# A two-batch model of six sublayers on one core: gate product of the feed-forward that runs beside the recurrence, moved from GpSimd to VectorE

## The reference

```python
x = x + 0.5 * ffn(layernorm(x))      # FFN0
x = x + mamba(layernorm(x))          # d_inner 512, d_state 16
x = x + 0.5 * ffn(layernorm(x))      # FFN1
x = x + 0.5 * moe(layernorm(x)); x = x + attention(layernorm(x)); x = x + 0.5 * moe(layernorm(x))

def ffn(x):                          # W1, W3: 1024 x 256, W2: 256 x 1024
    hidden = silu(x @ W1.T) * (x @ W3.T)
    return fwht(hidden) @ W2.T       # the transform is folded into W2 by the kernel
```

## Time and profile before

| | |
|---|---|
| runs | 899.51, 901.68, 901.64 us, median 901.64 |
| the profiled execution | 899.96 us, its span 897.9 us |
| TensorE busy | 761.5 us (85%) |
| VectorE busy | 570.1 us (63%) |
| ScalarE busy | 411.5 us (46%) |
| GpSimd busy | 270.1 us (30%) |
| mean granted clock of TensorE | 0.953 |

### The profile page before, as it was taken

The page is one execution under the profiler, slowest core; times in us unless marked ns, Lnnn a source line. Parts: engine busy times, 40 slices in busy tenths (PEclk is TensorE's granted clock), DMA queues, the critical chain, the costliest instruction groups (busy, mean ns, idle before and its releaser), DMA issues.

```text
span 897.9 us, 11226 instructions
## 1 busy us (share of the span) xinstructions
PE 761.5 (85%) x4027; PEld 531.3 (59%) x4027; DVE 570.1 (63%) x973; ACT 411.5 (46%) x606; POOL 270.1 (30%) x200
## 2 busy tenths in 40 slices
PE   3998868885793788898999999997789998685997
PEld 2688544552461355557787777774457785344776
DVE  4654698998959989984556556358524546713543
ACT  3455687664238466643332333440475431263221
POOL 0002069986503878980797000001000010000000
PEclk9999989998996989999999999999999999897999
DMA  9200011221101122215101000043000241000000
GB/s 297 76 1 1 2 58 59 82 71 59 47 1 49 58 59 75 79 59 155 63 2 20 1 1 1 13 108 93 4 1 1 66 115 32 28 1 0 1 1 24
DMA packets 30669, 41.88 MB, mean 47 GB/s; under 512 B 3817, under 2 KB 20019, under 8 KB 30579
## 3 DMA queue, kind: packets, MB, share of 16 engines
q1 hardware_dynamic: 29222, 40.41, 15.1%
q10 hardware_dynamic: 1396, 0.79, 0.4%
HBM read 36.83 MB, written 4.36 MB: 46 GB/s over the span
## 4 chain that ended last, share of the span: by engine, by line
PE 51%; DVE 16%; issue 14%; ACT 8%; DMA 5%; POOL 3%; SPq 2%; DVEq 0%; ACTq 0%; POOLq 0%
PE PS L462 34%; DVE PS L1706 3%; PE PS L776 2%; DVE shared L1714 2%; PE PS L912 2%; POOL shared L2014 2%; ACT shared L1332 2%; DMA route<-scratch_c 2%; PE PS L727 2%; PE PS L810 2%; DMA scratch_k<-shared 2%; ACT shared L1281 1%; DVE route L1765 1%; SPq L1953 1%; PE PS L655 1%
## 5 line engine op out<-in xcount | busy, mean ns | idle before, releaser
L2014 POOL TENSOR_TENSOR shared<-shared,route 128x1024 f32<-128x1024 f32 x64 | 151.8, 2376 | 105.0 <-DVE shared L1714 102.7
L462 PE MATMUL PS<-xnT,weights_r 128*128 128x256 f32 (+1 forms) x744 | 162.2, 365 | 11.3 <-ACT shared L1036 7.4
L462 PE MATMUL PS<-xnT,work_r 128*128 128x512 f32 (+1 forms) x624 | 159.1, 406 | 0.0
L462 PE MATMUL PS<-weights_r,work_r 128*128 128x256 f32 (+1 forms) x1008 | 147.3, 295 | 5.5 <-POOL work_r L1980 3.7
L1714 DVE TENSOR_TENSOR_SCAN shared<-shared,PS 128x512 f32<-128x512 f32 x128 | 148.8, 1203 | 4.0 <-POOL shared L2014 3.8
L462 PEld LDWEIGHTS PS<-xnT,weights_r 128*128 128x128 f32 x744 | 120.1, 194 | 46.1 <-issue 28.6
L462 PEld LDWEIGHTS PS<-weights_r,work_r 128*128 128x128 f32 (+1 forms) x1008 | 128.1, 191 | 24.5 <-issue 15.7
L1481 DVE TENSOR_TENSOR gated<-gated,PS 128x512 f32<-128x512 f32 (+1 forms) x68 | 46.6, 686 | 136.8 <-ACT gated L1016 136.8
L462 PEld LDWEIGHTS PS<-xnT,work_r 128*128 128x128 f32 (+1 forms) x624 | 115.8, 191 | 29.2 <-issue 1.1
L776 PE MATMUL PS<-shared,cf 128*128 128x512 f32 x256 | 128.0, 625 | 1.7 <-POOL shared L2014 1.7
L1016 ACT ACTIVATE gated<-PS 128x512 f32<-128x512 f32 (+1 forms) x68 | 40.6, 597 | 177.6 <-PE PS L462 170.7
(11 more groups left out here) (188 smaller groups left out, 949.9 us busy)
## 6 DMA issues: line engine op xcount, KB each, us to landing
route<-scratch_c SPq DMA_DIRECT2D x64, 256.0 KB, 3.1
shared<-in_L_ffn_W_dram SPq DMA_DIRECT2D x3, 1024.0 KB, 13.1
scratch_k<-shared SPq DMA_DIRECT2D x12, 128.0 KB
scratch_q<-shared SPq DMA_DIRECT2D x12, 128.0 KB
shared<-scratch_k SPq DMA_DIRECT2D x8, 192.0 KB
shared<-scratch_q SPq DMA_DIRECT2D x8, 192.0 KB
mamba_w<-in_L_ffn_w_dram SPq DMA_DIRECT2D x2, 704.0 KB, 5.2
beside<-in_L_ffn_w_dram SPq DMA_DIRECT2D x2, 704.0 KB, 7.9
```

The source lines that it names most:

```text
L462: last = nc.tensor.matmul(o, lhs[l], rhs[r], start=(start and i == 0), stop=(stop and i == 2))
L2014: nc.gpsimd.tensor_tensor(hc[:, u * 2 * T:(u + 1) * 2 * T].rearrange("p (c t) -> p c t", c=2), hst[:, (t % 2) * 2 * T:(t % 2 + 1) * 2 * T] ...
```

## The change

The gate product of all 16 units is done by VectorE, with the linear part read straight from bank 1. ScalarE's copy into `side_lin` and the tensor itself are gone. The SiLU counts a new semaphore `silu`, for which VectorE's product waits; TensorE's next unit waits for the product (`prod`) where it waited for the copy. The wait for the down product of unit i-2 moves from the copy to the rounding. VectorE's product stands at step u+2, ahead of that step's products and scans; for units 0 and 1 of the first phase it stands in front of and behind `norm_low`, and for the last two units where VectorE already had it. GpSimd keeps the remainders.

```diff
@@ TensorProgram.side_up
                 if r == 0:
                     pe.wait_ge(xnT_ev, 2 * it + 2)
-                    pe.wait_ge(f["lin"], b * UNITS + i)
+                    pe.wait_ge(f["prod"], b * UNITS + i)
@@ ScalarProgram
                 if i >= 2:
                     act.wait_ge(*side_done(b, i - 2, "hid"))
-                nc.scalar.activation(gated[:, (i % 2) * T:(i % 2 + 1) * T], bank(SIDE_GATE), ACT.Silu)
+                nc.scalar.activation(gated[:, (i % 2) * T:(i % 2 + 1) * T], bank(SIDE_GATE), ACT.Silu)\
+                    .then_inc(f["silu"], 1)
+
+            def side_high(self, b, i):
+
+                act, f = self.act, F
+                act.wait_ge(f["prod"], b * UNITS + i + 1)
                 if i >= 2:
                     act.wait_ge(*side_used(b, i - 2))
-                nc.scalar.activation(side_lin[i % RING], bank(SIDE_LIN), ACT.Copy).then_inc(f["lin"], 1)
-
-            def side_high(self, b, i):
-
-                act, f = self.act, F
-                act.wait_ge(*side_done(b, i, "prod"))
@@ VectorProgram.side_prod
-                self.dve.wait_ge(F["lin"], b * UNITS + i + 1)
-                nc.vector.tensor_tensor(g, g, side_lin[i % RING], ALU.mult).then_inc(F["prod_late"], 1)
+                self.dve.wait_ge(F["silu"], b * UNITS + i + 1)
+                nc.vector.tensor_tensor(g, g, bank(SIDE_LIN), ALU.mult).then_inc(F["prod"], 1)
@@ VectorProgram.mamba
                     self.norm(0, it + 1)
+                    self.side_prod(0, 0)
                     self.norm_low(it + 1, 0, banks=(2, 3))
+                    self.side_prod(0, 1)
                     self.taps(0, range(EC))
...
                 for t in range(STEPS):
+                    for i in range(2 * (1 - b), UNITS):
+                        if step_of(b, up_end(i)) + 2 == t:
+                            self.side_prod(b, i)
...
+                for i in range(ON_VECTOR):
+                    if step_of(b, up_end(i)) + 2 >= STEPS:
+                        self.side_prod(b, i)
@@ GpSimd, mamba
                     for i in range(2):
-                        side_prod(0, i)
                         side_low(0, i)
...
                         if step_of(b, up_end(i)) + 3 == t:
                             side_low(b, i)
-                        if step_of(b, up_end(i)) + 1 == t:
-                            side_prod(b, i)
```

More of the change, by code:

```diff
@@ L218, in build @@
         WoT, a = cut(shared, a, DC * D)
-        side_lin = [shared[:, RING_AT + i * 2 * T + T:RING_AT + (i + 1) * 2 * T] for i in range(RING)]
         ring = [halves(RING_AT + i * 2 * T, T)[0] for i in range(RING)]
@@ L330, in build @@
                                       "dA", "mul", "scan", "hc", "ys", "yr", "yf0", "yf"))
-        F = {n: sem(f"side_{n}") for n in ("up", "lin", "prod", "high", "hid", "used", "down", "res", "prod_late", "hid_late")}
+        F = {n: sem(f"side_{n}") for n in ("up", "silu", "prod", "high", "hid", "used", "down", "res", "hid_late")}
         SIDE_STAGE, SIDE_BATCH = (FFN0, FFN1), (1, 0)
@@ L1981, in side_low @@
                     .then_inc(f["hid"], 1)
-            def side_prod(b, i):
-                g = gated[:, (i % 2) * T:(i % 2 + 1) * T]
-                pool.wait_ge(F["lin"], b * UNITS + i + 1)
-                nc.gpsimd.tensor_tensor(g, g, side_lin[i % RING], ALU.mult).then_inc(F["prod"], 1)
             def mamba(b):
@@ L2034, in mamba @@
                     for i in range(ON_VECTOR):
-                        if step_of(b, up_end(i)) + 1 >= STEPS:
-                            side_prod(b, i)
                         if step_of(b, up_end(i)) + 3 >= STEPS:
```

## The result

| | before | changed |
|---|---|---|
| median of 4 runs each | 901.59 us | 913.19 us (912.50 to 915.44) |
| ratio | | 1.0123, 95% interval 1.0102 to 1.0144 |
| again, in a later set of runs | 903.50 us (23 runs) | 914.12 us (4 runs), ratio 1.0111 (1.0094 to 1.0128) |
| profiled execution, span | 899.96, 897.9 us | 915.44, 913.3 us |

The account below looks back on a forecast made before the run. VectorE was taken to bound the two step loops. The terms, -1.15 + 2.4 + 1.5 + 3.85 + 3.8 = +10.4 us, on the median of 901.64 gave 912.0 us, with 8 in 10 between 906 and 917.

Parts of the forecast that it names:

- Term 1: Before batch 0's loop: the rounding and the convolution's taps start earlier, -1.15 us.
- Term 2: Batch 0, steps 1 to 11: VectorE waits for two SiLUs, half repaid by vanished GpSimd waits, +2.4 us.
- Term 3: Batch 0, steps 12 to 31: three products add 1.8 us, GpSimd's earlier remainder gives 0.3 back, +1.5 us.
- Term 4: Batch 1's loop: unit 0's product delays TensorE by 0.86 us, five others cost 0.60 each, +3.85 us.
- Term 5: Batch 1's tail: TensorE waits for unit 6's product, +2.1 us, then half clock, +1.7 us; together +3.8 us.
- The clock holds: Rival: TensorE's idle time in the tail costs only itself, no clock loss; +8.7 us, 910.3 us, chance 0.16.
- Nothing behind the tail: Stages after the tail: bound by TensorE, nothing waits for a fixed time, so the shift stays; no further cost.
- The relief pays: Rival, whole kernel: SiLUs ready, TensorE's waits hidden, only prices count; +1.35 us, 903.0 us, no difference, chance 0.07.
- VectorE waits in every unit: Rival, both loops: nine other products each cost another 0.5 to 1 us waiting for ScalarE; about 919 us, chance 0.10.

Follow-up runs that it names:

- e11: Kernel before the change, with only batch 1's unit 6 product moved ahead of the residual: 903.71 us, ratio 1.0006.
- e9: Changed kernel with only unit 2's product of batch 0 one step later on VectorE: 911.38 us, ratio 1.0106.
- e4: Changed kernel with batch 1's units 0 to 5 back on ScalarE's copy and GpSimd's product: 908.64 us, ratio 1.0060.
- e6: Changed kernel, PSUM products only for batch 0 units 0-4, batch 1 units 6-7; units 2, 3 one step later, unit 6 ahead of residual: 899.83 us, ratio 0.9951.
- e7: Changed kernel, PSUM products only for batch 0 units 0, 1 and batch 1 units 6, 7, unit 6 ahead of the residual: 901.50 us, ratio 0.9975.
- e5: Changed kernel plus 16 unused TensorE matmuls of zeros during the tail's wait, ahead of unit 7's up pieces: 909.94 us, ratio 1.0074.
- e3: Changed kernel with batch 1's unit 6 product ahead of the residual and batch 0's units 2 and 3 one step later: 905.79 us, ratio 1.0021.
- e10: The e6 kernel with batch 0's unit 2 product one step later still, ahead of step 3: 902.00 us, ratio 0.9994.

## Why the prediction was right, point by point

- **Term 1, the start (-1.15):** -0.7 in both executions, -0.9 to -1.0 in most of the others, +0.2 in e11, which has the old route. The mechanism holds. Against the kernel before the size was a little high; against e11 the other executions are 1.0 to 1.3 us shorter, which is the forecast. e9, at -2.3, is the only execution without half clock in this stretch; all others have 3.4 us of it. In the changed kernel the second SiLU came 1.25 us later than in the earlier trace rows, where norm statistics 0.9 us late account for most.
- **Term 2, steps 1 to 11 (+2.4):** +2.3 in both. Foreseen were a wait of 5.0 us before step 1, scans at 125.24 there and at 141.2 in step 5, and at 162.3 in step 11; the trace has 4.87, 125.37, 141.33 and 162.43. The wait before step 5 was 0.92, not 1.6, because VectorE itself came 0.8 us later than forecast: it waited 0.55 us for TensorE's broadcast before step 4. The path of the second wait, GpSimd's work for the softplus behind the late scans, and ScalarE behind that, stands in the rows above (3.10 us for L395, which is L396 of before). The prediction told that wait as a consequence of the first one; e9 says that it comes without it too.
- **Term 3, steps 12 to 31 (+1.5):** +2.0, and +0.3 again. The three products cost 0.60 each in both; what differs between the two is the clock from step 24 on. VectorE's wait at step 24 fell by 0.46 us in the changed kernel (3.04 to 2.58), where 0.3 had been foreseen.
- **Term 4, batch 1's loop (+3.85):** +3.5, and +1.6 again. Five products at 0.60 are exact (e4). The first step's part, 0.86 for unit 0's product, holds too, once traces with the same clock are compared. The earlier trace rows stand at half clock: step 11 lasts 5.52 us there and 6.36 in the changed kernel, also at half clock. At full clock it lasts 4.62 to 4.63 in e4, e6, e7 and e11, which have the old route there, and 5.47 in the changed kernel's second execution. Both pairs differ by 0.84 to 0.85. What the prediction didn't see is that the 2.00 us wait of the earlier trace rows is made in part by half clock, so that a change of clock moves this stretch by up to 2.2 us, either way, in any of the kernels. VectorE's wait at step 11, in e11 and then in the changed kernel's second execution, both at full clock:

```profile
325.66 1.29 DVE L1706 TENSOR_TENSOR PS<-shared,PS 128x512 f32<-128x512 f32 x2 [1.10 <-PE PS L770]
```

```profile
328.07 1.29 DVE L1707 TENSOR_TENSOR PS<-shared,PS 128x512 f32<-128x512 f32 x2 [1.36 <-PE PS L769]
```

The wait grows by 0.26 and the product takes 0.60, together the 0.86. From 2.00 to 2.26 us it is the same at half clock. TensorE after the wait of the earlier trace rows, in e11 at full clock:

```profile
324.44 0.95 PE L462 MATMUL PS<-xnT,weights_r 128*128 128x256 f32 x6 [2.66 <-ACT shared L1036]
325.23 0.39 PE L770 MATMUL PS<-combT,cb 96*128 96x512 bf16 x1
```

- **Term 5, the tail (+2.1 of wait and +1.7 of clock):** +2.0 of wait (e5), and 1.6 or 2.6 of clock. "The clock holds" is refuted: none of the five executions with the wait and without e5's matmuls kept its clock. (The 0.50 that the prediction names stands in none of its rows: rows 10 give 0.57, a mean over 3.70 us. The window above has the 0.50.)
- **Nothing behind the tail:** here the step from the profiled execution to the median was weak. From FFN1 on the kernels don't differ, yet all twelve other profiled executions are 1.3 to 5.7 us longer there than that of the kernel before. The windows from FFN1 to the end, of the kernel before, of the changed one, of the changed one again and of e3:

```profile
427.00:897.80 470.80, 422.80 (x2554) 309.34 (x2553) 235.94 (x487) 172.37 (x253) 60.36 (x84) 0.96 0.10 27
```

```profile
441.20:913.20 472.00, 424.81 (x2554) 310.74 (x2552) 236.78 (x487) 172.69 (x253) 60.54 (x84) 0.95 0.09 24
```

```profile
435.50:911.10 475.60, 427.05 (x2549) 312.87 (x2552) 237.23 (x487) 172.36 (x253) 60.89 (x84) 0.95 0.09 24
```

```profile
428.40:904.80 476.40, 428.89 (x2549) 314.88 (x2552) 237.59 (x487) 172.71 (x253) 60.85 (x84) 0.94 0.10 27
```

The longer, the lower the mean clock, and the more busy time for the same matmuls. The execution on which the sum was made had a favourable clock there. So 910.4 for the profiled execution missed 915.44 by 5 us, while 912.0 for the median missed 913.19 by 1.2.
- **Luck in the number:** the stretches of the five terms come to +11.5 us in the changed kernel's first profiled execution and to +7.0 in its second, against +10.4 forecast, and the stretches that the sum held at nothing add 3.9 and 6.3. The mechanisms are shown one by one; that their sum fell within 1.2 us of the median is in part luck, since single executions of the kernel before alone range over more than 5 us. The bounds given for the terms add up to some 7 to 15 us, not to 16.

- **A term that was missing:** between the loops the changed kernel loses 1.7 us. Eight executions of twelve have this, among them e7 and e11, which have no new product in the loops, and the changed kernel again doesn't. It is the clock, and not the change. Changed, then again:

```profile
242.49 5.30 PE L775 MATMUL PS<-shared,cf 128*128 128x512 f32 x8
```

```profile
241.25 3.60 PE L775 MATMUL PS<-shared,cf 128*128 128x512 f32 x8
```

- **"The relief pays"** had the right arithmetic for a kernel with another order: it was said to decide if unit 2's SiLU were in time and unit 6's product could pass the residual. With both repaired (e3) the ratio is 1.0021, which is 903.5 us on 901.6, against the 903.0 of that rival.
- **"VectorE waits in every unit"** didn't happen: all products of units 4 to 7 and of batch 1's loop ran without a wait.

The Trainium skill (VectorE: DVE Perf Modes, on the TRN2 errata) has a PSUM source cost 62 cycles more than one from SBUF. Measured with the same operation and size: 669 ns with one operand in PSUM (x16, 658 to 689), 688 with both in SBUF (x2). The trace doesn't agree, and leaving the rule out of the sum was right.

## What to carry to other kernels

Before an instruction is moved to another in-order queue, look at three times in the trace of before: when its input is ready, when the new engine gets to the slot, and who is queued behind it. Here the price of an instruction (0.60 us) was less than the two waits that its place made (4.9 and 4.1 us). One step later 1.4 us of the first were left, and ahead of the residual the second was gone. Too late costs as well, when another engine's queue waits for the result (e10).

Moving work from an engine with room to the full one pays as far as the full one waited for the other: units 2 to 4 of batch 0 gained 2.5 us net by the traces (e6 against e7; 1.7 by the medians), three later ones and five in batch 1's loop cost 0.60 us each. A split by place (e6) beat all on either engine.

A difference of one trace against another holds, stage by stage, only where a second trace repeats it. Where the clock may differ, compare traces at the same clock: unit 0's 0.84 us shows in both such pairs, while mixed pairs differ by -0.1 to +1.7 us at that step.

## What the runs showed of the hardware

The granted clock of TensorE doesn't follow from the program alone. In the changed kernel, behind unit 0's product in batch 1's loop, six matmuls took 1.62 us at half clock in one execution and 0.94 at full clock in the other, after the same wait:

```profile
329.81 1.62 PE L461 MATMUL PS<-xnT,weights_r 128*128 128x256 f32 x6 [3.49 <-DVE gated L1494]
```

```profile
326.86 0.94 PE L461 MATMUL PS<-xnT,weights_r 128*128 128x256 f32 x6 [3.50 <-DVE gated L1494]
```

So it is between two kernels: after the same wait of 2.66 us, at the same place of the same code, TensorE ran six matmuls in 1.62 us at half clock in the kernel before and in 0.95 us in e11. After the wait of 4.1 us in the tail half clock lasted 3.4 us in three executions and 6.8 us in two. In sum TensorE's half clock was 86.6 us in the profiled execution of before, 112.9 and 107.0 in those of the changed kernel, but 103.0 in e6, the fastest kernel, and 106.9 in e11. The mean clock was 0.953 before and 0.940 in the changed kernel, but also 0.942 in e11: for the most part that is a difference between executions, not the change. Over 23 later executions of the kernel before it had a median of 0.944 (0.938 to 0.951), over the four of the changed one beside them 0.939 (0.935 to 0.943). The kernel before itself ranged from 899.85 to 905.23 us over 23 runs on one chip.
